# Statistics, transposes and splits of the first feed-forward pair moved up into the last attention turns

## The chip, the cores and the metric

One core of a Trainium2 chip. The time is device microseconds of one execution of the whole kernel; the median of the runs shown is compared.

## What is computed

A decoder layer on x of 4 x 2048 tokens of 512 numbers, in float32:

```python
x = x + s5(layernorm(x))                    # a linear recurrence over the 4 batch rows
x = x + cross_attention(layernorm(x), ctx)  # 16 heads, 77 context tokens for each batch row
x = x + ffn(layernorm(x))                   # 512 -> 2048, butterfly, gelu, butterfly, 2048 -> 512
```

The butterfly factors are folded into the two weight matrices of the feed-forward part while the kernel runs. Every product is made of three products of split operands: a high part that the tensor engine can take, and the low rest.

## The kernel before

The tokens are worked in NG = 16 groups of 512 (T = 4 tiles of 128 tokens). Three phases follow each other: the recurrence, attention and the feed-forward part.

**Attention** is software-pipelined in turns g = 0 to 17. Turn g makes scores and exponentials of group g, the values and half of the output projections of group g-1, the other half of group g-2, and the transposes and queries of group g+1. Each engine has its own list for a turn, written out by hand: attn_pe (TensorE, called PE), attn_act (ScalarE, ACT), attn_dve (VectorE, DVE), norm (GpSimd, POOL), and a list of DMAs on SyncE (SP). An engine works its list strictly in order, and waits on semaphores where it needs another. In turn 15 the last scores are made. Turn 16 has no scores: it has values(0) to values(3) and project(0), project(1) of group 15, and project(2), project(3) of group 14. Turn 17 has only project(2) and project(3) of group 15 with their residual additions.

Results of PE pass through four PSUM banks, 4 to 7, by slot numbers: slot n lies in bank 4 + n % 4, and PE waits until DVE has finished the slot that had the bank before (semaphore dve_slot). ACT copies the high part out (hi), DVE subtracts it and writes the low part (lo). Scores use banks 0 to 3. So values(2), slot 12, waits for lo_v(0), slot 8; turn_p(0), slot 14, waits for lo_v(1), slot 10; project(0), slot 18, waits for the low part of slot 14; project(3) (slot 7) waits for residual(2), slot 3, in the same bank.

For each tile t of group g: scores(t) on PE, shift(t) on DVE (two maxima and a subtraction), exp(t) on ACT, sums(t) on DVE (sum and reciprocal), norm on POOL, then turn_p(t) on PE (transposes), hi_p and lo_p.

**The feed-forward part** works the groups in pairs p = 0 to 7. Before its first product a pair needs: load_x2 of both groups into X; stats3(0), stats3(1) (DVE, LayerNorm statistics, L1149 and L1161 to L1167); rsqrt (POOL, L694 and L696); apply3(0), apply3(1) (ACT, L814); turn3(0) to turn3(7) (PE, 4 transposes each, L1737); raw_x(0) to raw_x(7) (ACT, L930), copying them to rawx; and seven operand splits in the order B11, T3, T2, B21, B22, T4, T1: hi_x3 (ACT, L935), lo_x3 (DVE, L1178), with mix_x (DVE, L1322) ahead of T3, T2, T4, T1. Each mix_x needs a split before it, and each hi_x3 of a mixed operand needs its mix_x. Then the products up(0, c, j) read weights from a ring of seven buffers (load_ring, L612). The third of them, A12, writes to a bank of which ACT must first have copied the first product (U, L1066), and this copy stands behind all seven hi_x3 in ACT's list.

For p = 0 all of this stands in turns 16 and 17. In turn 16 each engine works the stats, applies and transposes between its attention steps; the split of B22 comes ahead of residual(2) of turn 17 on DVE, the splits T4 and T1 come behind residual(3) of turn 17.

**Weights of the feed-forward part** are made on the way: turn g mixes, splits and stores one of 16 sets (load_wc, mix_weights L1308 and L1314, high_weights L939, low_weights L1178, store_wc L586 and L587) through one buffer pair, so that each load waits for the store before. The last set, 15, is made in turn 16. The operands B22, T4 and T1 lie where this buffer pair was, so that ACT waits for wc_stored of set 15 ahead of them; before the change ACT waits so ahead of all seven.

SP works one list as well: near the end store_x2(16), store_wc(15), a wait until that is stored, a wait for the last values, seven load_ring, store_x2(17).

## Time and profile before

| | |
|---|---|
| median of 3 runs | 2364.82 us (2364.71 to 2370.11) |
| the profiled execution | 2366.6 us, span 2364.8 us |
| TensorE busy | 2226.1 us, 94% of the span |
| VectorE busy | 1769.8 us, 75% |
| ScalarE busy | 1293.1 us, 55% |
| GpSimd busy | 557.2 us, 24% |
| attention turns 15 to 17 | about 966 to 1055 us of the span |
| first feed-forward products | from 1055 us |

PE's busy time counts matmuls whatever the clock. The granted clock (PEclk) is given as a share of full speed: 1.00 is 2.4 GHz, 0.50 is 1.2 GHz. Lines of the time line give the start in us from the span's start, the duration in us, the engine, the line, the operation with its operands, how often, and in brackets how long the engine stood idle before it and who ended the wait.

### The profile page before, as it was taken

Reading aid. Unit: us, or ns where it says so; the run is one execution under the profiler, and the core shown is the slowest. Engines: PE = TensorE matmul, PEld = TensorE weight load, DVE = VectorE, ACT = ScalarE, POOL = GpSimd, SP = SyncE. Lnnn points to the kernel's source line nnn. Section 1 sums busy time; section 2 is a strip of 40 time slices with the busy share of each in tenths; the row PEclk is TensorE's granted clock in tenths of the full one; section 3 lists DMA queues with packets and bytes.
Section 4 is the critical chain, followed back from the end, with each engine's and each line's share of the span. In section 5 each row is a group of like instructions: output and inputs, shape, how many; then the busy total and the mean of one; then the engine's idle time right before and its main releaser. Section 6 shows DMA issues by size and latency. Waiting matters only on the chain.

```text
span 2364.8 us, 42243 instructions
## 1 busy us (share of the span) xinstructions
PE 2226.1 (94%) x15752; PEld 1943.3 (82%) x15752; DVE 1769.8 (75%) x2969; ACT 1293.1 (55%) x2832; POOL 557.2 (24%) x619
## 2 busy tenths in 40 slices
PE   8877789999999999969999999999999999999998
PEld 4777668778777877748998998988989989989898
DVE  5999668878878887755875867857858758678567
ACT  2998556666667666543644635535536446355343
POOL 3788222222222322200030030020210300300203
PEclk9888879999999999989999999999999999999999
DMA  8555702332332232256568677676685686776765
GB/s 329 192 178 189 263 2 77 116 124 77 108 116 94 85 119 90 95 182 219 172 219 267 199 218 227 208 262 179 212 263 177 214 266 200 223 221 210 225 188 177
DMA packets 190883, 424.47 MB, mean 179 GB/s; under 512 B 27342, under 2 KB 64718, under 8 KB 190286
## 3 DMA queue, kind: packets, MB, share of 16 engines
q1 hardware_dynamic: 190696, 421.94, 55.1%
q8 instruction: 121, 1.98, 0.3%
q14 instruction: 66, 0.54, 0.1%
HBM read 331.29 MB, written 90.60 MB: 178 GB/s over the span
## 4 chain that ended last, share of the span: by engine, by line
PE 65%; DVE 16%; ACT 11%; issue 4%; DMA 3%; POOL 1%; SPq 0%; DVEq 0%; ACTq 0%; POOLq 0%
PE ps L416 52%; PE ps L1805 5%; ACT es L982 5%; PE ps L1773 2%; DVE gl L1178 2%; DVE G L1530 2%; DVE st L1149 2%; DVE ptl L1178 1%; DVE wc_s L1178 1%; PE ps L1784 1%; DMA xa<-in_x 1%; DVE rsum L1401 1%; ACT wc_h L939 1%; DVE rmax L1390 1%; ACT pth L957 1%
## 5 line engine op out<-in xcount | busy, mean ns | idle before, releaser
L416 PE MATMUL ps<-ring,gh 128*128 128x256 f32 x3584 | 654.4, 285 | 12.6 <-DVE gl L1178 12.5
L416 PEld LDWEIGHTS ps<-ring,gh 128*128 128x128 f32 x3584 | 558.0, 192 | 16.9 <-DVE gl L1178 15.7
L416 PE MATMUL ps<-xth,ring 128*128 128x512 f32 x1792 | 554.6, 390 | 4.2 <-ACT U L1066 4.2
L416 PE MATMUL ps<-ring,gl 128*128 128x256 f32 x1792 | 506.8, 283 | 0.0
L416 PEld LDWEIGHTS ps<-xth,ring 128*128 128x128 f32 x1792 | 337.4, 188 | 74.7 <-issue 4.6
L1054 ACT ACTIVATE gh<-G 128x512 fp32r<-128x512 f32 x384 | 237.2, 629 | 212.4 <-PE ps L416 212.1
L416 PE MATMUL ps<-xtl,ring 128*128 128x512 f32 x896 | 349.5, 390 | 0.0
L416 PEld LDWEIGHTS ps<-ring,gl 128*128 128x128 f32 x1792 | 343.4, 192 | 0.0
L1178 DVE TENSOR_TENSOR gl<-G,gh 128x512 fp32r<-128x512 f32 x384 | 278.8, 739 | 57.2 <-ACT gh L1054 55.6
L759 POOL TENSOR_TENSOR es<-es,rinv 128x308 f32<-128x308 f32 x256 | 180.2, 735 | 456.5 <-DVE rinv L1405 456.5
L1470 DVE TENSOR_TENSOR U<-ps,U 128x512 f32<-128x512 f32 (+1 forms) x168 | 137.3, 817 | 169.5 <-PE ps L416 166.9
L1037 ACT ACTIVATE G<-G,up_b 128x512 f32<-128x512 f32 x192 | 139.2, 725 | 222.1 <-DVE G L1470 222.1
L1470 DVE TENSOR_TENSOR G<-ps,U 128x512 f32<-128x512 f32 x192 | 132.8, 692 | 123.5 <-PE ps L416 122.9
L694 POOL TENSOR_TENSOR rstd<-var_e,mhalf 128x4 f32<-128x4 f32 x48 | 55.2, 1150 | 629.1 <-DVE var_e L1167 629.1
L416 PEld LDWEIGHTS ps<-xtl,ring 128*128 128x128 f32 x896 | 168.8, 188 | 34.9
L982 ACT ACTIVATE es<-ps,rmax 128x77 f32<-128x77 f32 x512 | 157.9, 338 | 60.0 <-DVE rmax L1390 60.0
L786 POOL TENSOR_TENSOR X<-X,U 128x256 f32<-128x256 f32 x64 | 72.7, 1166 | 488.4 <-DVE U L1470 488.4
L416 PE MATMUL ps<-woh,aoh 128*128 128x512 f32 x256 | 107.8, 421 | 16.0 <-DVE x L1381 12.5
L1784 PE MATMUL ps<-ident,es 128*128 128x128 f32 (+1 forms) x768 | 104.0, 284 | 19.7 <-POOL es L759 6.3
L1037 ACT ACTIVATE G<-ps,up_b 128x512 f32<-128x512 f32 x64 | 44.2, 690 | 136.7 <-PE ps L416 136.7
L957 ACT ACTIVATE pth<-ps 128x512 fp32r<-128x512 f32 x128 | 69.7, 597 | 87.7 <-PE ps L1784 87.7
L775 POOL TENSOR_TENSOR X<-X,ob 128x512 f32<-128x512 f32 x64 | 86.2, 1379 | 127.0 <-DMA X<-x_scratch 113.2
(212 smaller groups left out, 4646.0 us busy)
## 6 DMA issues: line engine op xcount, KB each, us to landing
ring<-wup_scratch SPq DMA_DIRECT2D x224, 512.0 KB, 3.8
ring<-wdn_scratch SPq DMA_DIRECT2D x224, 512.0 KB, 3.6
X<-x_scratch SPq DMA_DIRECT2D x32, 1024.0 KB, 8.5
xa<-in_x SPq DMA_DIRECT2D x16, 1024.0 KB, 5.5
x_scratch<-xa SPq DMA_DIRECT2D x16, 1024.0 KB, 4.3
x<-x_scratch SPq DMA_DIRECT2D x16, 1024.0 KB, 5.6
x_scratch<-x SPq DMA_DIRECT2D x16, 1024.0 KB, 4.3
out_x<-X SPq DMA_DIRECT2D x16, 1024.0 KB, 6.3
```

The source lines that it names most:

```text
L416: mm = pe.matmul(bank, a, b, start=first and i == 0, stop=last and i == n - 1, skip_group_check=go_on)
L759: mul = nc.gpsimd.tensor_tensor(e[:, f], e[:, f], r[:, f].unsqueeze(2).broadcast_to([P, HPC, L]), ALU.mult)
L775: x = tt(X[:, i * T + t, :], X[:, i * T + t, :], ob[:, :], ALU.add)
L786: ins = tt(x, x, U[:, u + t // 2, t % 2 * HW:(t % 2 + 1) * HW], ALU.add)
L957: his.done(A(out, bank, ACT.Copy), hi_slot(n))
L982: e = A(es[t % 2][:, f, h * L:(h + 1) * L], ps[:, h, f * LP:f * LP + L], ACT.Exp, bias=rmax[:, t % 2, at:at + 1], accum_out=rsum[:, t % 2, ...
L1037: A(dst, dst if src is None else src, ACT.Gelu, bias=up_b[:, chunk:chunk + 1]).then_inc(gelu_done, 1)
L1054: A(gh[e % GR][:, :], src, ACT.Copy).then_inc(g_hi, 1)
L1178: sub = lambda o, a, b: V.tensor_tensor(o, a, b.bitcast(F32), ALU.subtract)
L1470: add = lambda o, a, b: V.tensor_tensor(o, a, b, ALU.add)
L1784: mm = pe.transpose(b[0:keys.shape[1], j * P:(j + 1) * P], keys, ident[:, :])
L1805: mm = pe.matmul(b[0:VW[c]], v[:, f, V_AT[c]:V_AT[c + 1]], pt, start=(i == 0), stop=(i == len(passes) - 1))
```

## The change

The order on five engines is changed; no operation is added or dropped.

- Turn 15: DVE has stats3(0) behind residual(3) and stats3(1) behind sums(1). ACT has apply3(0) behind hi_v(1) and apply3(1) behind high_weights. POOL has its two rsqrt behind the norms of tiles 0 and 1.
- Turn 16, PE: turn3(0) to turn3(3) come first of all, turn3(4) to turn3(7) behind project(2). ACT: raw_x(0) to raw_x(3) ahead of hi_p(2), raw_x(4) to raw_x(7) ahead of hi_p(3), the splits B11 and T3 ahead of hi_v(0), T2 ahead of hi_v(1), high_weights right behind hi_v(1), B21 behind hi_v(3), then the wait for wc_stored, then B22, T4, T1. DVE: the low parts of B11 and T3 and two mix_x ahead of lo_v(0), T2 ahead of lo_v(1), B21 behind residual(0), B22 behind residual(1); T4 and T1 stay behind residual(3) of turn 17.
- SP: the seven load_ring are issued ahead of store_wc(15) and the wait for its end.

```diff
--- before.py
+++ after.py
@@ -621,11 +621,11 @@
             store_wc(NG - 2)
             load_wc(NG - 1)
             store_x2(NG)
-            store_wc(NG - 1)
-            sp.wait_ge(wc_stored, 32 * NG)
             sp.wait_ge(pe_slot, SLOTS * NG + V_SLOT[-1] + 1)
             for n in range(RING):
                 load_ring(n)
+            store_wc(NG - 1)
+            sp.wait_ge(wc_stored, 32 * NG)
             store_x2(NG + 1)
             sp.dma_start(ob[:, :], bcon).then_inc(ob_loaded, 16)
             sp.dma_start(ob2[:, :], dbias).then_inc(ob_loaded, 16)
@@ -758,12 +758,14 @@
                     for f in range(KC):
                         mul = nc.gpsimd.tensor_tensor(e[:, f], e[:, f], r[:, f].unsqueeze(2).broadcast_to([P, HPC, L]), ALU.mult)
                     mul.then_inc(p_ready, 1)
+                    if g == NG - 1 and t == 0:
+                        rsqrt(2 * NG, xn2_ready, NG)
+                    if g == NG - 1 and t == 1:
+                        rsqrt(2 * NG + 1, xn3_ready, 1)
 
             attn_loop(pool, norm)
 
 
-            rsqrt(2 * NG, xn2_ready, NG)
-            rsqrt(2 * NG + 1, xn3_ready, 1)
             tt = nc.gpsimd.tensor_tensor
             pool.wait_ge(ob_loaded, 32)
             tt(ob[:, :], ob[:, :], ob2[:, :], ALU.add).then_inc(ob_ready, 1)
@@ -986,31 +988,43 @@
                         e = es[t % 2][:, :, 0:HB * L]
                         A(e, e, ACT.Exp).then_inc(exp_done, 1)
 
+                if g == NG:
+                    for i in range(4):
+                        raw_x(0, i, i)
                 hi_p(2, -1)
+                if g == NG:
+                    for i in range(4, 8):
+                        raw_x(0, i, i - 4)
                 hi_p(3, -1)
                 exp(0)
                 if has(1) and not (isinstance(g, int) and g == 0):
                     apply2(g + 1)
                 if g == NG:
                     load_table(ACT.Gelu)
-                    apply3(0)
+                    act.wait_ge(x2_stored, 16 * (NG - 2))
+                    hi_x3(0, B11)
+                    hi_x3(0, T3)
                 hi_v(0)
                 hi_x(0)
                 if g == NG:
-                    apply3(1)
+                    hi_x3(0, T2)
                 exp(1)
                 hi_v(1)
+                if g == NG:
+                    high_weights(g - 1)
+                if g == NG - 1:
+                    apply3(0)
                 hi_x(1)
                 hi_v(2)
                 hi_v(3)
-                if 1 <= g <= NG:
+                if 1 <= g < NG:
                     high_weights(g - 1)
+                if g == NG - 1:
+                    apply3(1)
                 if g == NG:
-                    for i in range(8):
-                        raw_x(0, i, i % 4)
-                    act.wait_ge(x2_stored, 16 * (NG - 2))
+                    hi_x3(0, B21)
                     act.wait_ge(wc_stored, 32 * NG)
-                    for o in SPLIT_ORDER:
+                    for o in SPLIT_ORDER[4:]:
                         hi_x3(0, o)
                 if isinstance(g, int) and g == 0:
                     for j in range(4):
@@ -1408,22 +1422,25 @@
                 if has(1) and not (isinstance(g, int) and g == 0):
                     moments2(g + 1)
                 residual(2, -2)
-                if g == NG:
-                    stats3(0)
                 shift(0)
                 lo_p(3, -1)
                 sums(0)
                 residual(3, -2)
+                if g == NG - 1:
+                    stats3(0)
                 if g == NG:
-                    stats3(1)
-                if g == NG + 1:
-                    split_first(5, PROD)
+                    split_first(0, 2)
+                    mix_x(0, 1)
                 shift(1)
                 lo_v(0)
                 lo_x(0)
                 if 1 <= g <= NG:
                     mix_weights(g - 1)
                 sums(1)
+                if g == NG - 1:
+                    stats3(1)
+                if g == NG:
+                    lo_x3(0, T2)
                 lo_v(1)
                 lo_x(1)
                 lo_v(2)
@@ -1442,10 +1459,12 @@
                 sums(2)
                 lo_x(3)
                 if g == NG:
-                    split_first(0, 3)
+                    split_first(3, 4)
                 residual(1, -1)
                 if g == NG:
-                    split_first(3, 5)
+                    split_first(4, 5)
+                if g == NG + 1:
+                    split_first(5, PROD)
                 lo_p(1, 0)
                 shift(3)
                 lo_q(0)
@@ -1816,9 +1835,18 @@
                     slots.done(split3(pe, bank(O_SLOT[t]), [(aoh[:, f, tok], aol[:, f, tok], woh[:, f, :], wol[:, f, :])
                                                             for f in range(KC)]), O_SLOT[t])
 
+                if g == NG:
+                    pe.wait_ge(e_ready, T * NG)
+                    pe.wait_ge(exp_ps, T * NG)
+                    for i in range(4):
+                        turn3(0, i, i)
                 turn_p(2, -1)
                 project(2, -2)
                 scores(0)
+                if g == NG:
+                    for i in range(4):
+                        pe.wait_ge(x3_raw, i + 1)
+                        turn3(0, 4 + i, i)
                 turn_p(3, -1)
                 project(3, -2)
                 start = isinstance(g, int) and g == 0
@@ -1832,20 +1860,11 @@
                     scores(1)
                 values(2)
                 values(3)
-                if g == NG:
-                    pe.wait_ge(e_ready, T * NG)
-                    pe.wait_ge(exp_ps, T * NG)
-                    for i in range(4):
-                        turn3(0, i, i)
                 turn_p(0, 0)
                 scores(2)
                 turn_x(2)
                 project(0, -1)
                 turn_x(3)
-                if g == NG:
-                    for i in range(4):
-                        pe.wait_ge(x3_raw, i + 1)
-                        turn3(0, 4 + i, i)
                 project(1, -1)
                 turn_p(1, 0)
                 scores(3)
```

## Rows read from the trace of the kernel before

**Rows 1.** The page: shares of the chain that ended last
```profile
PE 65%; DVE 16%; ACT 11%; issue 4%; DMA 3%; POOL 1%; SPq 0%; DVEq 0%; ACTq 0%; POOLq 0%
```
**Rows 2.** Time line of PE, turns 15 to 17 (start, us, operation, idle before)
```profile
988.61 1.50 PE L1784 MATMUL ps<-ident,es 128*128 128x128 f32 x12 [2.85 <-DVE aol L1178]
...
1008.94 2.82 PE L1784 MATMUL ps<-ident,es 128*128 128x128 f32 x12 [4.74 <-POOL es L759]
...
1024.75 1.94 PE L1737 MATMUL ps<-ident,X 128*128 128x128 f32 x16
...
1049.89 0.79 PE L416 MATMUL ps<-woh,aoh 128*128 128x512 f32 x1 [12.53 <-DVE x L1381]
...
1062.64 0.69 PE L416 MATMUL ps<-xth,ring 128*128 128x512 f32 x1 [4.22 <-ACT U L1066]
```
**Rows 3.** Chain that ended last, in order of time, 1000 to 1055 (start, us, what)
```profile
1000.42 0.81 DVE rmax L1390
...
1002.98 0.84 ACT es L982 x5
...
1030.44 6.46 DMA wdn_scratch<-wc_s
...
1036.97 1.07 ACT xth L935
...
1039.29 1.15 DVE rawx L1322
...
1048.02 1.22 DVE xtl L1178
1049.24 0.61 DVE x L1381
...
1049.89 5.50 PE ps L416 x12
```
**Rows 4.** Time line of DVE, turns 15 and 16
```profile
980.93 0.68 DVE L1178 TENSOR_TENSOR aol<-ps,aoh 128x512 fp32r<-128x512 f32 x1
985.04 1.68 DVE L1308 TENSOR_TENSOR wc_s<-wc_s 128x256 f32<-128x256 f32 x4 [3.43 <-DMA wc_s<-wd_scratch]
...
989.90 1.29 DVE L1178 TENSOR_TENSOR ptl<-ps,pth 128x512 fp32r<-128x512 f32 x2 [0.25 <-ACT pth L957]
...
1008.90 2.46 DVE L1149 BATCH_NORM_STATS2 st<-X 128x6 f32<-128x512 f32 x4
...
1012.29 1.28 DVE L1178 TENSOR_TENSOR ptl<-ps,pth 128x512 fp32r<-128x512 f32 x2
```
**Rows 5.** Time line of ACT, one apply3 of turn 16
```profile
1013.88 2.94 ACT L814 ACTIVATE X<-X,nmr,rstd 128x512 f32<-128x512 f32 x4
```
**Rows 6.** DMA issues with us to landing, asked at 967.6, 1030.4 and 1040.0
```profile
wdn_scratch<-wc_s SPq DMA_DIRECT2D x1, 896.0 KB, 13.2
...
wdn_scratch<-wc_s SPq DMA_DIRECT2D x1, 896.0 KB, 6.5
...
ring<-wup_scratch SPq DMA_DIRECT2D x1, 512.0 KB, 8.4
```
**Rows 7.** Time line of SP's queue
```profile
966.04 0.92 SPq L605 DMA_DIRECT2D X<-x_scratch  x2
...
1036.92 3.34 SPq L612 DMA_DIRECT2D ring<-wup_scratch  x7
```
**Rows 8.** One stretch of 1 us: PE, PEld, DVE, ACT, POOL busy times, PEclk, DMA share, GB/s
```profile
1047.00:1048.00 1.00, 0.00 (x0) 0.00 (x0) 1.00 (x1) 0.01 (x1) 0.00 (x0) 0.50 0.44 172
```
**Rows 9.** Time line of PE, pauses of earlier turns
```profile
329.07 2.15 PE L1784 MATMUL ps<-ident,es 128*128 128x128 f32 x9 [2.55 <-DVE ptl L1178]
521.41 0.76 PE L1805 MATMUL ps<-pth,vh 128*128 128x512 f32 x1 [3.35 <-issue]
```
**Rows 10.** Stretches of 1 us, as rows 8: the clock behind two pauses
```profile
989.00:990.00 1.00, 1.00 (x11) 0.84 (x8) 0.75 (x3) 0.73 (x2) 1.00 (x3) 1.00 0.00 0
...
1013.00:1014.00 1.00, 1.00 (x4) 0.81 (x3) 0.97 (x2) 0.99 (x3) 0.77 (x2) 0.50 0.03 8
```

## The prediction

> **What bounds the kernel.** I read the page first: PE is busy for 94% of the span (in the table above) and holds 65% of the chain that ended last [rows 1]. So an edit is worth only what it does to PE's pauses and to its clock. I then read PE's time line over the turns that the diff touches. There the reader sees a pause of 2.85 us in turn 15, one of 4.74 us at 1008.94, one of 12.53 us at 1049.89 that DVE's residual addition ended, and one of 4.22 us at 1062.64 that ACT's copy U ended [rows 2]. These are what the change can win. The chain of this stretch [rows 3] tells why the long one exists: the store of weight set 15 lands at 1036.90, then come five splits in turns of ACT and DVE, the last low part at 1048.02 and residual(2) of turn 17 at 1049.24, and only then may project(3) start in the same bank. It starts at 1049.89 and takes 5.50 us, at half clock. Third come the clock and the DMA rows, since both are about to be loaded differently.
>
> What decides is the start of this last project(3). Behind it nothing is moved: it ends at 1055.39, residual(3), mix_x, T4, mix_x, T1 and U follow, and the third product starts at 1062.64 [rows 2, 3], 7.25 us later. From there on PE runs the same work as before. So the effect of the whole change is the shift of that start.
>
> **Turn 15, what is added.** One stats3 holds DVE from 1008.90 to 1012.29, 3.39 us [rows 4]. The first sits ahead of shift(1), so lo_v(0), at 980.93 before, comes 3.4 us later. values(2) had followed it at once and now waits some 3.3 us. mix_weights stood idle for its DMA until 985.04 [rows 4] and absorbs the lateness of DVE: this DMA does not move. The second stats3 has no such cover: it sits between sums(1) and lo_v(1), and turn_p(0) waits for the latter [rows 2], so 988.61 becomes 992.0. ACT now has two apply3 of 2.94 us [rows 5] in turn 15, the second ahead of hi_p(0). Its statistics end at 991.3, POOL's rsqrt takes some 1.3 us more, apply3(1) ends at 995.5, and hi_p(0) and lo_p(0), which was at 989.90 [rows 4], come at 996.1: 6.2 us late. project(0) and shift(2) wait for that. Slack in the rest of the turn returns some 0.7 us. I get the end of scores(3) at 1005.4, where it was at 1000.0: 5.4 us late. The X loads are issued at 966.04 [rows 7] and landed long before DVE wants them.
>
> **Turn 16.** The first turn3 use the scores' banks and so wait for exp(3): from its maximum to the last exponential out of these banks tile 3 took from 1000.42 to 1003.82, 3.4 us [rows 3]. PE stands from 1005.3 to 1008.7, 3.4 us. The old order had turn_p(2) and project(2) there and then 4.74 us of pause for the norm of tile 3 [rows 2]; that pause is gone, since 16 transposes (1.94 us [rows 2]), turn_p(2), project(2) and again 16 transposes cover it. With 1.4 us for a turn_p (1.50 with its tail [rows 2]) and 2.8 for a project (half of the 5.50 at half clock [rows 3]), values(0) starts at 1020.8, against 1015.9. Next is values(2): it waits for lo_v(0), behind B11, mix_x, T3, mix_x. Table load until 1020.2, then 1.07 (hi) + 1.22 (low) + 1.15 (mix) + 1.07 + 1.22 + 1.15 [rows 3] and about 1 for aoh and aol: 1028.1. PE pauses 3.6 us, and values(3) ends at 1032.0, where it ended at 1024.8: 7.2 us late. The last low_weights ends at 1035.4 instead of 1029.8, 5.6 us late.
>
> **The DMA order.** This is the step that I think decides. SP issues the seven ring loads at 1032.0 and needs 3.34 us [rows 7], then at 1035.4 the stores of set 15. In the trace, the seventh ring load was issued at about 1040.0 and landed 8.4 us later [rows 6], 1048.3; the DMA share of 0.44 in the microsecond of 1047 [rows 8] puts the last of their bytes at about 1047.4, 10.5 us behind the first issue. Does a store queued behind them wait for them? At 967.6 the trace has that very case: set 13's store was queued behind the two X loads of 966.04 and took 13.2 us to land, against 6.5 us when nothing was ahead of it [rows 6, 7]. So it waits. Alone, the second half of the store landed 6.46 us behind its issue [rows 3] and the whole 7.1 us behind the first; of that about 1.1 us passed before bytes moved, as an estimate from the ring loads (issued at 1036.92, done 10.5 us later), so 6.0 us are left behind a full queue. wc_stored then comes at 1032.0 + 10.5 + 6.0 = 1048.5. Before it was 1036.90: 11.6 us later, although its data are only 5.6 us later.
>
> The Trainium skill (DMA: Bandwidth & Descriptors, section Queues, rings and completion order) says that each DMA engine takes the descriptors of one ring in order and shares its time only between different queue rows. That speaks against this change, as the landing of 13.2 us does.
>
> **What the splits give back.** Four of seven splits are now out of the way early, but B22 still waits for wc_stored and still stands ahead of residual(2) of turn 17. So 1048.5 + 1.1 (hi) + 1.2 (low) + 0.7 (residual and issue) gives project(3) at 1051.5; carried through with the same small issue gaps as before, the shift against 1049.89 lies between +1.4 and +2.2 us. I take +2. The pause ahead of it is about 9.5 us instead of 12.53, and the clock is low behind it in both. The ends of this term: were the store as fast as at 1030.44 (7.1 us from issue), project(3) would start at 1045.5, -4.4 us; with a receipt as slow as at 967.6, +3.3 us.
>
> **The clock.** Removed is the half clock behind the pause of 4.74 us: turn_p(3) took 2.82 us instead of 1.50 [rows 2] and the clock was still 0.50 at 1013 [rows 10]. That saving is already in my times above, which are all at full clock. Added are two pauses where PE then sets the pace, 3.4 us at 1008.7 and 3.6 us at 1028.1. Pauses of 2.55 and 3.35 us were followed by half clock: nine transposes took 2.15 us [rows 9], where twelve take 1.50 [rows 2], and a first matmul of values 0.76; one of 2.85 us was not, twelve took 1.50 and the clock at 989 was 1.00 [rows 2, 10]. Behind 1008.94 the clock was still 0.50 at 1013 [rows 10], in all some 6 us; so a pause costs between 0 and 3 us. I take 1.7 for each, 3.4 in all: something past the middle, since two of the three pauses of this size brought half clock. In turn 15 the pauses lie under DVE's lateness and cost at most 0.7 us.
>
> The Trainium skill (TensorE: Matmul & The Clock Gate, section What's actually happening) says that the monitor behind the clock runs free of the kernel, so whether a given pause costs anything is partly chance. By that the two terms are 0 or full; the sum would be +2, +3.7 or +5.4 us.
>
> **The sum.** +2.0 + 3.4 = +5.4 us on the profiled execution: span 2364.8 to 2370.2, time 2366.6 to 2372.0. The median of the runs is 2364.82, so 2370.2 there. A measurement of this kernel can tell some 0.3%, 7.1 us, from no change; the forecast lies inside.
>
> **Rivals.**
> - *The store is not held up* (for: it is a smaller transfer, and some of its bytes may overtake; against: the 13.2 us of rows 6). Then B22 is split at 1045 and project(3) starts 4.4 us earlier than before, less the 0 to 3.4 us of clock: 2360.4 to 2363.8. Chance 0.15.
> - *The pauses cost more* (slower): each of the two at 1008.7 and 1028.1 leaves the clock at 0.50 for 6 us, as at 1008.94, and turn 15's 0.7 us counts: 2.0 + 6.0 + 0.7 = +8.7, 2373.5. It decides once half clock outlasts 5 us behind each pause. Chance 0.25.
> - *Turn 15 hides the statistics*: DVE had 3.43 us of idle ahead of mix_weights [rows 4], and if hi_p(0) is not the late one, scores(3) is only 1 to 2 us late. T3 and T2 come earlier, the ring loads start 4 us earlier, and everything behind them: -4 + 5.4, 2366 or, with full clock, 2363. Chance 0.1.
> - *The change pays as it looks*: both of the above together, the 12.53 us pause falls to 2 or 3 us: about -9, 2356. Chance 0.05.
> - My forecast, 2368 to 2372: 0.45.
>
> The range drops the last rival and the far end of the second: 2360 to 2375. Faster by over 0.3%: 0.07; within: 0.63; slower: 0.30.
>
> **What would show it.** Right: scores(3) of group 15 ends 4 to 6 us later; DVE's BATCH_NORM_STATS2 lies ahead of the second and behind the second shift of turn 15; ring loads are issued at about 1032 to 1036, the stores of set 15 land 12 to 14 us after their issue; the long pause of PE is still ahead of a projection, ended by DVE's addition, some 9 us, and ACT stands about 15 us for that DMA. Wrong: a landing of 7 us for these stores, project(3) starting before 1047, full clock behind the pauses of 3.5 us, or turn_p(0) of turn 15 ahead of 990.

## The result, and the profile after

The changed kernel takes 2373.97 us in the median of six runs (2370.83 to 2375.76), against 2366.30 us for six runs of the kernel before beside it (2364.62 to 2370.11). The ratio is 1.0028, 95% interval 1.0015 to 1.0040: slower by 0.28%, just below what I had called the limit of what can be told. A second set of runs of the same kernel, with 17 runs of the kernel before beside it, gave 2374.5 us and 1.0038 (1.0025 to 1.0050). So by the medians the change costs 7.7 and 8.4 us; the two intervals reach from 3.5 to 12 us. The forecast was 2370.2 us, between 2360 and 2375. It was worked out from 2364.82 us, the median of three runs of the kernel before; from the 2366.30 of six the same shift of 5.4 us gives 2371.7.

The page of the changed kernel: busy times, and the chain's shares. No busy time has moved by more than 1.3 us, and PE's by 0.3 (rows 1 had the chain), so the eight microseconds are nearly all waiting.

```profile
span 2373.0 us, 42244 instructions
PE 2226.4 (94%) x15752; PEld 1942.0 (82%) x15752; DVE 1769.4 (75%) x2969; ACT 1292.3 (54%) x2832; POOL 556.3 (23%) x619
PE 64%; DVE 17%; ACT 9%; issue 4%; DMA 4%; DVEq 0%; SPq 0%; POOL 0%; ACTq 0%; POOLq 0%
```

PE's time line of the changed kernel, to be laid beside [rows 2] (start, duration, operation, idle before it and who ended it). The line numbers have moved: L1803 is turn_p, L1756 turn3, L1824 values.

```profile
985.06 0.50 PE L1824 MATMUL ps<-pth,vh 128*128 128x512 f32 x1 [2.98 <-DVE aol L1192]
...
992.13 1.50 PE L1803 MATMUL ps<-ident,es 128*128 128x128 f32 x12 [3.12 <-DVE aol L1192]
...
997.15 0.67 PE L416 MATMUL ps<-woh,aoh 128*128 128x512 f32 x1 [2.05 <-DVE ptl L1192]
...
1011.16 3.47 PE L1756 MATMUL ps<-ident,X 128*128 128x128 f32 x16 [3.91 <-issue]
...
1056.99 0.80 PE L416 MATMUL ps<-woh,aoh 128*128 128x512 f32 x1 [10.06 <-DVE x L1395]
...
1069.62 0.77 PE L416 MATMUL ps<-xth,ring 128*128 128x512 f32 x1 [4.50 <-ACT U L1080]
```

The pause of 4.74 us has gone and three shorter ones, of 2.98, 3.12 and 2.05 us, have come in turn 15, one of 3.91 us at the head of turn 16, and (not shown) one of 3.52 us ahead of values(2). The long pause is still ahead of the last project(3), still ended by DVE's addition, 10.06 us instead of 12.53. The third product starts at 1069.62, 6.98 us later than before. The span is 8.2 us longer. Turn 15 starts at 965.8 to 965.9 in both traces, and from the third product to the end they take 1302.2 and 1303.4 us, so all but 1.2 us of it lies in this stretch. PE's pauses in the stretch (those the time line shows, 0.4 us and more) add up to 32.1 us, where they were 26.4: 5.7 of the 6.9 us. The rest is work that took longer.

The chain that ended last, of the changed kernel, against [rows 3] (start, duration, what):

```profile
1040.53 0.56 SPq L586
1041.09 0.04 issue
1041.13 12.87 DMA wdn_scratch<-wc_s
1054.03 1.06 ACT xth L937
1055.12 0.03 DVE xtl L1192
1055.15 1.11 issue
1056.26 0.69 DVE x L1395
1056.95 0.04 issue
1056.99 5.39 PE ps L416 x12
```

The store's 6.46 us have become 12.87, and between it and project(3) there is now one split where there were five.

### The profile page after: what moved, and what is told of

It is laid out like the page before. It is cut to its first block, busy times and chain, and to the rows that moved or that the text cites. A ratio compares the mean times of both kernels' runs of the same rounds, so it can differ in the third digit from the quotient of the medians.

```text
span 2373.0 us, 42244 instructions
## 1 busy us (share of the span) xinstructions
PE 2226.4 (94%) x15752; PEld 1942.0 (82%) x15752; DVE 1769.4 (75%) x2969; ACT 1292.3 (54%) x2832; POOL 556.3 (23%) x619
## 4 chain that ended last, share of the span: by engine, by line
PE 64%; DVE 17%; ACT 9%; issue 4%; DMA 4%; DVEq 0%; SPq 0%; POOL 0%; ACTq 0%; POOLq 0%
PE ps L416 52%; PE ps L1824 5%; ACT es L984 5%; DVE st L1163 2%; PE ps L1792 2%; DVE gl L1192 2%; DMA xa<-in_x 2%; DVE G L1549 2%; DVE ptl L1192 2%; DMA x_scratch<-xa 1%; PE ps L1803 1%; DVE wc_s L1192 1%; DVE rsum L1415 1%; DVE rmax L1404 1%; ACT pth L959 1%
## 5 line engine op out<-in xcount | busy, mean ns | idle before, releaser
L416 PEld LDWEIGHTS ps<-ring,gh 128*128 128x128 f32 x3584 | 558.0, 192 | 16.9 <-DVE gl L1192 15.6
L416 PEld LDWEIGHTS ps<-xth,ring 128*128 128x128 f32 x1792 | 338.0, 189 | 75.4 <-issue 4.9
L416 PE MATMUL ps<-woh,aoh 128*128 128x512 f32 x256 | 107.6, 420 | 16.6 <-DVE x L1395 10.1
L1803 PE MATMUL ps<-ident,es 128*128 128x128 f32 (+1 forms) x768 | 102.4, 281 | 15.1 <-DVE xt2l L1192 5.7
```

The source lines that it names most:

```text
L416: mm = pe.matmul(bank, a, b, start=first and i == 0, stop=last and i == n - 1, skip_group_check=go_on)
L1803: mm = pe.transpose(b[0:keys.shape[1], j * P:(j + 1) * P], keys, ident[:, :])
```

## The experiments

Single traces differ in where turn 15 starts (962.8 to 965.9 us), so I read each trace from the start of its turn_p(2) of turn 15, called 0 here. "Landed" is the landing of the store of set 15, "third" the start of the third product (where the copy U is early, the pause is at another product, and no number is given). The experiments were run in three sets; the median of the kernel before beside them was 2366.00, 2366.23 and 2366.12 us, and 2366.30 beside the changed kernel's first.

| kernel | scores(3) end | landed | third | median us | ratio to before (95%) |
|---|---|---|---|---|---|
| before | 34.2 | 71.1 | 96.8 | 2366.0 to 2366.3 | 1 |
| changed | 41.4 | 88.1 | 103.8 | 2373.97 | 1.0028 (1.0015 to 1.0040) |
| store first | 41.2 | 81.4 | 96.1 | 2365.5 | 0.9998 (0.9987 to 1.0008) |
| B22 late | 41.2 | 88.0 | 96.8 | 2368.13 | 1.0006 (0.9996 to 1.0016) |
| ring first alone | 37.6 | 80.8 | 106.5 | 2373.24 | 1.0026 (1.0014 to 1.0039) |
| statistics alone | 41.2 | 75.4 | 100.4 | 2370.82 | 1.0022 (1.0013 to 1.0032) |
| both orders | 41.3 | 81.4 | 93.1 | 2362.80 | 0.9986 (0.9978 to 0.9995) |
| residuals first | 34.1 | 70.6 | 93.5 | 2364.64 | 0.9994 (0.9986 to 1.0003) |
| statistics placed | 40.7 | 88.0 | 103.7 | 2374.18 | 1.0038 (1.0024 to 1.0051) |
| placed, both orders | 40.6 | 81.5 | 93.1 | 2362.25 | 0.9985 (0.9976 to 0.9993) |
| placed, both orders, U early | 40.6 | 81.4 | - | 2359.89 | 0.9974 (0.9965 to 0.9984) |
| before, residuals first, U early | 34.2 | 70.7 | - | 2359.60 | 0.9974 (0.9963 to 0.9985) |
| changed, again | 41.6 | 90.0 | 104.6 | 2374.50 | 1.0038 (1.0025 to 1.0050) |

**1. The store ahead of the ring loads again.** The changed kernel with one edit on SP:

```diff
-            sp.wait_ge(pe_slot, SLOTS * NG + V_SLOT[-1] + 1)
-            for n in range(RING):
-                load_ring(n)
             store_wc(NG - 1)
             sp.wait_ge(wc_stored, 32 * NG)
+            sp.wait_ge(pe_slot, SLOTS * NG + V_SLOT[-1] + 1)
+            for n in range(RING):
+                load_ring(n)
```

> The changed kernel with SP's old order: store of weight set 15 and the wait for it ahead of the seven ring loads. Theory (the store queued behind the ring loads decides the end): the stores are issued when low_weights ends, about 1040.5, and land in 7.1 us instead of 13, at 1047.6; B22, residual(2) follow, the last project(3) starts at 1050.6 instead of 1057.0, the third product 6.4 us earlier; 6 to 7 us faster than the changed kernel, 0 to 2 us slower than the kernel before. Rival (the chain of splits or the clock holds project(3) back whatever the store does): no change against the changed kernel, 7 to 8 us slower than before.

Measured: 2365.5 us, 8.5 us less than the changed kernel and level with the kernel before. Its chain, in the same form as above:

```profile
1040.83 6.43 DMA wdn_scratch<-wc_s
...
1047.29 1.06 ACT xth L937
...
1049.52 0.69 DVE x L1395
...
1050.25 4.46 PE ps L416 x12
```

The second half of the store takes 6.43 us instead of 12.87; project(3) starts at 1050.25 where 1050.6 was expected. The low weights are ready at nearly the same time in both kernels (DVE ends them at 1040.15 here and at 1040.43 there; the first half of the store is issued at 1040.23 and 1040.53), so the 6.4 us are the place in the queue and nothing else. The third product starts 7.7 us earlier than in the changed kernel: the rest is mostly project(3), which took 4.46 us here and 5.39 there. The rival is out.

**2. B22 behind the last residual.** The changed kernel with one edit on DVE:

```diff
-                if g == NG:
-                    split_first(4, 5)
                 if g == NG + 1:
-                    split_first(5, PROD)
+                    split_first(4, PROD)
```

> The changed kernel with the low part of B22 behind residual(3) of turn 17 instead of ahead of residual(2); SP's new order is kept, so the store still lands late, about 1054. Theory (what costs is that residual(2), and with it project(3), stands behind a split that waits for the store): project(3) follows project(2) without a pause at 1047, full clock; PE's pause moves behind the first two products, which end near 1053; B22, T4, T1 and U follow the store in some 9 us, so the third product starts at about 1063 instead of 1069.6: 6 to 7 us faster than the changed kernel. Rival (the end is the store's landing plus a fixed chain): the third product stays at 1068 to 1070 and nothing is gained.

Measured: 2368.13 us, 5.8 us less than the changed kernel. In PE's time line the pause has moved from project(3) to the third product:

```profile
1045.93 0.50 PE L416 MATMUL ps<-woh,aoh 128*128 128x512 f32 x1 [0.85 <-DVE x L1395]
...
1061.11 0.76 PE L416 MATMUL ps<-xth,ring 128*128 128x512 f32 x1 [9.41 <-ACT U L1080]
```

From the store's landing to the third product it takes 8.8 us; in the changed kernel it takes 15.6, since project(3) stood in between. The store was as late as before. So the late store costs what it does because two residuals stand behind a split that needs it.

**3. The ring loads first, alone.** The kernel before with the edit of experiment 1 the other way round.

> The kernel before with only SP's new order: seven ring loads ahead of the store of set 15. Theory (DMA queue in order): ring loads are issued at 1024.9 when the last values end, the store is issued at 1029.8 and lands some 16.8 us behind the first ring load, at 1041.7 instead of 1036.9; all seven splits, project(3) and the third product come 4.8 us later: +5 us on the whole. Rival (the queue shares its time between transfers): the store lands as before or within 2 us, +0 to +2 us.

Measured: 2373.24 us, 7.2 us slower than before: the SP order by itself costs as much as the whole change. DMA issues of this kernel, asked at 1031.5 and 1032.1 (KB, us to landing):

```profile
wdn_scratch<-wc_h SPq DMA_DIRECT2D x1, 896.0 KB, 11.3
wdn_scratch<-wc_s SPq DMA_DIRECT2D x1, 896.0 KB, 13.2
```

From the first ring load at 1026.57 to the landing at 1045.28 it took 18.7 us, 1.9 more than in the changed kernel and more than the 16.8 I had expected. In the microseconds from 1043 and 1044 only 24 and 23 GB/s were moved, where it had been about 385 before; why the end of the store dragged here is not shown. The rival, a queue that shares its time, forecast a landing at most 2 us later and is out. The changed kernel's own trace agrees: its seventh ring load, issued at 1040.05, landed 9.2 us later, against 8.4 us with no store behind it [rows 6], and the store landed 4.8 us after that.

The trace of experiment 3 also has a thing that has nothing to do with the edit: its turn 15 is 3.4 us longer than in the trace of before, though the instructions are the same. PE's time line and two stretches show why (in each stretch: its length, the busy time of PE, PEld, DVE, ACT and POOL with their instructions, then the granted clock, the DMA share and GB/s):

```profile
987.52 1.50 PE L1784 MATMUL ps<-ident,es 128*128 128x128 f32 x12 [3.09 <-DVE aol L1178]
```

```profile
988.00:989.00 1.00, 1.00 (x14) 0.80 (x12) 0.75 (x2) 0.82 (x2) 1.00 (x3) 0.94 0.00 0
...
992.00:993.00 1.00, 1.00 (x3) 0.81 (x3) 1.00 (x2) 0.37 (x3) 0.00 (x0) 0.50 0.00 0
```

The pause was 3.09 us here and 2.85 us there [rows 2], and here 1.2 GHz followed it for some 7 us, where there the clock stayed at 2.4 GHz [rows 10]. Of these 3.4 us 2.9 are left where the store is issued (67.0 us from the start of turn 15, against 64.0), so some 3 of this trace's 9.7 us at the third product come from the clock in turn 15, and 6.7 are the order.

**4. The statistics in turn 15, alone.** The kernel before with the moves on DVE, ACT and POOL that bring the statistics forward, and nothing else (the added lines; the same calls are taken out of turn 16):

```diff
@@ POOL, turn 15
+                    if g == NG - 1 and t == 0:
+                        rsqrt(2 * NG, xn2_ready, NG)
+                    if g == NG - 1 and t == 1:
+                        rsqrt(2 * NG + 1, xn3_ready, 1)
...
@@ ACT
                 hi_v(1)
+                if g == NG - 1:
+                    apply3(0)
...
                     high_weights(g - 1)
+                if g == NG - 1:
+                    apply3(1)
...
@@ DVE
                 residual(3, -2)
+                if g == NG - 1:
+                    stats3(0)
...
                 sums(1)
+                if g == NG - 1:
+                    stats3(1)
```

> The kernel before with only the statistics, rsqrt and apply3 of both groups moved into turn 15; transposes, splits and SP's order stay. Theory (turn 15 is paced by DVE and ACT, which is what the statistics load): the end of scores(3) of group 15 moves from 1000.0 to 1007.2, as in the changed kernel; turn 16 wins back some 2 us since apply3(1) no longer stands ahead of high_weights; the store lands at about 1042 and the third product starts 4 to 6 us later: +5 us. Rival (the statistics hide beside DMA waits and slack of turn 15): scores(3) at most 2 us later, and a gain of 1 to 3 us on the whole.

Measured: 2370.82 us, 4.8 us slower. scores(3) ends 7.0 us later, as in the changed kernel, so turn 15's whole lateness is the statistics. Turn 16 gives back a little more than expected (the store lands 4.3 us later, the third product starts 3.6 us later, where 4 to 6 had been forecast). The rival is out.

**5. Both orders.** Experiments 1 and 2 in one kernel.

> The changed kernel with both repairs: SP stores set 15 ahead of the ring loads, and B22 is split behind residual(3) of turn 17. Theory (the store's late landing and the residuals behind it are one chain, and what is left after the first repair is the store's own landing plus hi B22, mix, T4, mix, T1, U): the store lands at 1047.3 as in the first repair; from the landing to the third product the second repair took 8.8 us, so it starts at 1056.1 instead of 1062.0; 6 us faster than the first repair alone, 6 to 7 us (0.3%) faster than the kernel before. Rival (the two repairs remove the same wait and do not add): no more than 1 us better than the better of the two.

Measured: 2362.8 us, 2.7 us less than with the first repair alone and 3.4 us (0.14%) less than before, where 6 to 7 were expected. The third product starts 3.0 us earlier than with the first repair, not 6. What I had overlooked is in PE's time line:

```profile
1047.21 0.50 PE L416 MATMUL ps<-woh,aoh 128*128 128x512 f32 x1 [0.85 <-DVE x L1395]
...
1050.65 0.50 PE L416 MATMUL ps<-xth,ring 128*128 128x512 f32 x1 [0.40 <-DMA ring<-wup_scratch]
...
1058.64 0.76 PE L416 MATMUL ps<-xth,ring 128*128 128x512 f32 x1 [4.97 <-ACT U L1080]
```

B22's low part stands behind residual(3), and residual(3) waits for project(3), which ends at 1050.25. In experiment 2 the store landed after that, and the 8.8 us began with the landing; here the landing is at 1047 and the chain begins with project(3), so 3 of the 6 us are taken back. The chain that ended last says the same: it runs through project(3) and residual(3), and the store is no longer in it.

**6. Residuals first in the kernel before.** One edit on DVE: of the seven splits only the first stays ahead of the residuals of turn 17.

```diff
                 residual(3, -2)
...
                 if g == NG + 1:
-                    split_first(5, PROD)
+                    lo_x3(0, T3)
+                    split_first(2, PROD)
...
-                if g == NG:
-                    split_first(0, 3)
                 residual(1, -1)
                 if g == NG:
-                    split_first(3, 5)
+                    split_first(0, 1)
+                    mix_x(0, 0)
```

> The kernel before with one edit: on DVE the two residual additions of turn 17 come right behind the first split and mix_x, and the other six splits behind them. Theory (the pause of 12.53 us before the last project(3) is owed to the order on DVE alone, not to statistics or transposes): project(3) follows project(2) at about 1039 after some 1 to 2 us of pause instead of 12.5, the splits run on beside it, the third product starts at about 1056 instead of 1062.6; 6 to 7 us faster than the kernel before. Rival (the chain of seven splits is as long as the pause, so nothing is won by letting project(3) go): within 2 us of before.

Measured: 2364.64 us, 1.6 us less than before, and the interval (0.9986 to 1.0003) takes in no change. The trace's third product is 3.3 us earlier. project(3) has its pause cut from 12.53 to 3.68 us, but the second product now waits 4.14 us for T2 and the third 6.41 us for U. So the rival was right on the time, but the trace gives another reason than its own. The edit puts both residuals ahead of the splits, and residual(3) waits for project(3). So the splits did not run on beside project(3), as I had expected; the chain that ended last goes through all of it:

```profile
1039.84 4.61 PE ps L416 x12
...
1044.54 0.12 DVE x L1381
...
1045.15 1.22 DVE xtl L1178
```

Up to 1044.54 DVE was idle for 4.76 us, and ACT for 7.25 us up to its next split, while the third product waited for the splits that DVE had still to work. It is the same wait as in experiment 5. An order with only residual(2) ahead of the splits and residual(3) behind some of them was not tried.

**7. The statistics in other places of turn 15.** The changed kernel; stats3(0) into DVE's wait for the weights, stats3(1) behind the low parts that free PE's banks, apply3(1) behind hi_p(0).

```diff
                 residual(3, -2)
-                if g == NG - 1:
-                    stats3(0)
...
                 lo_x(0)
+                if g == NG - 1:
+                    stats3(0)
                 if 1 <= g <= NG:
                     mix_weights(g - 1)
                 sums(1)
-                if g == NG - 1:
-                    stats3(1)
...
                 lo_v(3)
+                if g == NG - 1:
+                    stats3(1)
...
@@ ACT
-                if g == NG - 1:
-                    apply3(1)
...
                 hi_p(0, 0)
+                if g == NG - 1:
+                    apply3(1)
```

> The changed kernel with the statistics in other places of turn 15: stats3(0) ahead of mix_weights, where DVE stood 3.4 us idle for a DMA, stats3(1) behind lo_v(3), apply3(1) behind hi_p(0). SP's order and the splits stay as changed. Theory (turn 15's 7 us are owed to where the statistics and apply3(1) stand, not to their amount): the end of scores(3) comes back from 1007.2 to about 1003.5, and all behind it 3 to 4 us earlier: 3 to 4 us faster than the changed kernel. Rival (DVE and ACT are full in turn 15, any place costs the same 6.8 us): no change.

Measured: 2374.18 us, no change against the changed kernel; scores(3) ends 0.7 us earlier in the trace, not 3 to 4. PE's time line:

```profile
985.38 1.06 PE L1803 MATMUL ps<-ident,es 128*128 128x128 f32 x8 [2.72 <-DVE aol L1192]
...
987.85 1.06 PE L1803 MATMUL ps<-ident,es 128*66 128x128 f32 x4 [1.40 <-DVE aol L1192]
...
992.52 0.76 PE L416 MATMUL ps<-woh,aoh 128*128 128x512 f32 x1 [0.90 <-DVE ptl L1192]
```

The pauses are shorter, 5.0 us in three instead of 8.2. The clock took nearly all of it back. It fell at 987, behind the first of them, and stayed at 0.50 for some 10 us, where the changed kernel had it so for some 3 us from 997 on. So the transposes of turn_p(0) took 2.1 us instead of 1.5, scores(2) 2.79 instead of 1.54, project(0) and project(1) 8.11 instead of 7.32: from the start of turn 15 to the end of scores(3) PE's work took 2.4 us more in all, against 3.1 us less pause, and 0.7 us are left. In the traces of experiments 8 and 9, which have the same places, the pauses, the 10 us of half clock and the end of scores(3) (40.6) are the same. My theory was that the place and not the amount costs the time. The place did change the pauses; in the time it gained nothing.

**8. All three repairs.** Experiments 5 and 7 in one kernel.

> All three repairs in the changed kernel: statistics in the idle places of turn 15, store ahead of the ring loads, B22 behind residual(3) of turn 17. Theory (the causes are independent and add): third product 3 to 4 us earlier than with the two orders repaired, 9 to 10 us (0.4%) faster than the kernel before, 16 to 18 us faster than the changed kernel. Rival (once the store is not late, turn 16's own chain takes over): no better than the two orders alone.

Measured: 2362.25 us, as experiment 5 (2362.8). That is 4.0 us less than before and 11.7 less than the changed kernel, where 9 to 10 and 16 to 18 had been forecast. The other places of the statistics give nothing here either: scores(3) ends 0.7 us earlier than in experiment 5, the store lands at the same time (81.5 against 81.4), and so does the third product start (93.1). The rival held.

**9. The copy U early.** Experiment 8, and on ACT the high parts of T4 and T1 behind the copy U in the first round of the products.

```diff
-                    for o in SPLIT_ORDER[4:]:
+                    for o in SPLIT_ORDER[4:5]:
                         hi_x3(0, o)
...
                     A(U[:, 2 - 2 * (c % 2)], ps[:, 4 * (c % 2) + UP_BANK[A11], :], ACT.Copy).then_inc(first_copied, 1)
+                    if p == 0 and c == 0:
+                        for o in SPLIT_ORDER[5:]:
+                            hi_x3(0, o)
```

> The version with all three repairs, and on ACT the copy U of the first product (on which the third product waits) ahead of the high parts of T4 and T1 instead of behind them. Theory (after the repairs what PE waits for longest is the copy U, 4.7 us, which stands behind the chain of splits only by its place in ACT's list): the third product starts some 0.5 us after the second ends, two products (2.7 us) are made while T4 and T1 are split, and the fifth waits for T1 till about 59.5 where it was at 61.1: 1.5 to 2.5 us faster than the three repairs alone. Rival (the last split T1 is needed by the fifth product at about the time at which it is ready anyway): within 0.5 us of it.

Measured: 2359.89 us, 2.4 us less than experiment 8 and 6.2 us (0.26%, interval 0.16 to 0.35%) less than the kernel before. Four products run through without a stop, and the pause, now 2.96 us, is ahead of the fifth.

**10. The copy U and the residuals, in the kernel before.** Experiment 6 with the edit of experiment 9.

> The kernel before with the residuals of turn 17 first on DVE, and with the copy U ahead of the high parts of T4 and T1 on ACT; statistics, transposes and SP's order as before. Theory (the whole gain that was in this stretch lies in two places of the order, and none in moving the statistics): the pause of 6.4 us ahead of the third product shrinks, the fifth product starts some 2 us earlier than with the residuals alone: 5 to 6 us faster than the kernel before, as good as the changed kernel with all its repairs. Rival (without the early statistics and splits the chain of seven splits is the bound and the copy gives nothing): as with the residuals alone, 1 to 3 us faster than before.

Measured: 2359.6 us, 6.5 us less than the kernel before, level with experiment 9, which has the statistics, transposes and splits moved, the three repairs and the same copy. Its time line of PE:

```profile
1040.76 0.50 PE L416 MATMUL ps<-woh,aoh 128*128 128x512 f32 x1 [3.69 <-DVE x L1384]
...
1050.90 0.50 PE L416 MATMUL ps<-xth,ring 128*128 128x512 f32 x1 [4.14 <-DVE xtl L1181]
...
1060.30 0.47 PE L416 MATMUL ps<-xth,ring 128*128 128x512 f32 x1 [3.41 <-issue]
```

The lines are the last project(3), the second product and the fifth. DVE waits for project(3) here as in experiment 6, 4.77 us. Against experiment 6 the median gains 5.0 us, more than the 2 us that the chain was expected to give. There a pause of 6.41 us was followed by half clock, here one of 3.41 us was not. One stretch of each (numbers as in experiment 3), experiment 6 first. It is one trace of each, so that the clock makes up the difference is likely and not shown.

```profile
1061.00:1062.00 1.00, 1.00 (x4) 0.81 (x3) 0.00 (x0) 0.43 (x1) 0.00 (x0) 0.50 0.00 0
```

```profile
1061.00:1062.00 1.00, 1.00 (x5) 0.69 (x5) 0.65 (x2) 0.00 (x0) 0.00 (x0) 1.00 0.00 0
```

**11. The changed kernel again.**

> The changed kernel itself once more, on the chip and in the rounds of the two others, for an interval of its own and a second trace. Expected: 7 to 8 us slower than the kernel before; the store behind the ring loads lands 12 to 13 us after its issue again; the pauses of 3.0, 3.1 and 3.5 us in turns 15 and 16 are there at the same places, but which of them is followed by half clock differs from the first trace. Rival (the half clock behind each pause is fixed by the program): the same stretches at 0.50 as in the first trace.

Measured: 2374.5 us, 8.4 us more than the kernel before beside it, ratio 1.0038. The second half of the store landed 12.8 us after its issue. The pauses are at the same places. Ahead of turn_p(0) of turn 15 the pause is 3.55 us, followed by half clock, where it was 3.12 us and full clock. scores(2) then took 2.78 us instead of 1.54, but the next pause shrank from 2.05 to 0.46 us, and the clock was half at project(0) in both traces; scores(3) ends at 41.6 and 41.4. Ahead of values(2) of turn 16 the pause is 3.54 us (3.52 in the first trace). The clock was still 1.00 in the first microsecond behind it and half for some 3.5 us after that, so values(2) and values(3) took 5.5 us, no less than the first trace's 5.4. So the rival fell, but the draw changed little in the time.

```profile
992.00:993.00 1.00, 1.00 (x12) 0.59 (x14) 0.00 (x0) 1.00 (x3) 0.00 (x0) 0.50 0.00 0
...
1031.00:1032.00 1.00, 0.41 (x2) 0.37 (x3) 0.97 (x3) 0.97 (x2) 0.00 (x0) 1.00 0.00 0
```

## Why the prediction was right, and where it was off

The direction, the mechanism and the range held; the size was 5.4 us forecast against 7.7 measured. The narrower band that I held most likely, 2368 to 2372, was missed: the median is 2 us above it. Of the signs that were to show the forecast right, the store's landing (13.5 us behind its issue, 12 to 14 forecast), the long pause (10.06 us, some 9) and ACT's wait for the DMA (15.37 us, about 15) came; scores(3) ended 7.2 us late, where 4 to 6 had been said, and the ring loads were issued at 1037.2, outside 1032 to 1036. None of the signs for wrong came.

The shift of the third product can be taken apart by the traces of before and after, both read from the start of turn 15:

| term | before | after | difference | forecast |
|---|---|---|---|---|
| turn 15 start to store issued | 64.0 | 74.7 | +10.6 | +9.0 (5.6 + 3.4 for the clock) |
| store issued to landed | 7.1 | 13.5 | +6.4 | +6.0 |
| landed to third product | 25.7 | 15.6 | -10.1 | -10.0 |
| sum | 96.8 | 103.8 | +6.9 | +5.4 |

The three terms of the forecast sum to +5.0 and not to its +5.4, because it took +2 for a shift that its own terms put at 1.6 without the clock. Against +6.9 its sum is 1.5 us too small, and the first term accounts for that.

- **Turn 15, the amount.** Forecast 5.4 us at the end of scores(3), measured 7.2. The steps behind it held: values(2) waited 2.98 us (about 3.3 forecast), turn_p(0) started at 992.13 (992.0), hi_p(0) at 995.70 and lo_p(0) at 996.31 (996.1), and project(0) started at 997.15, right behind. What was mis-sized is the clock in turn 15, which the forecast put at 0.7 us at most and left out of its sum. Behind the pause of 2.05 us ahead of project(0) the clock was at 0.50 at 998, and project(0) and project(1) took 7.32 us instead of the 5.7 that they took before: 1.6 us. I had looked at each pause alone and taken the last one, 2 us, for too short; three pauses in 15 us were not the same thing. It was no bad luck of one trace: in all six traces with the statistics in these places the clock was half at project(0), whichever of the pauses it had fallen behind, the two projections took 7.1 to 7.3 us, and scores(3) ended at 41.2 to 41.6. Experiment 4 confirms that the whole lateness is the statistics.
- **Turn 16.** The pause ahead of the first turn3 was 3.91 us (3.4 forecast), the one ahead of values(2) 3.52 (3.6). Both were followed by half clock, as assumed: 16 transposes took 3.47 us instead of 1.94, and values(2) and values(3) 5.4 instead of 4.0. Together 2.9 us, where 3.4 had been taken. Here I had weighed two outcomes for each pause; all eight traces that have these two pauses show half clock behind both.
- **The DMA order.** Forecast: landing 16.5 us behind the first ring load. Measured 1054.0 - 1037.2 = 16.8. Experiment 1 shows that the price of the order is 6.4 us at the landing, 7.7 us at the third product and 8.5 us in the medians, experiment 3 that the order costs 7.2 us with nothing else changed. That is shown, not only argued.
- **What the splits give back.** Shown by experiment 1: with the store issued 10.3 us later than before it still reaches the third product 0.8 us earlier. In round numbers the moved splits are worth 10 us of chain; the statistics that make them possible cost 7, turn 16's own pauses 3, the store's place 6.
- **The rival "the pauses cost more"** stood at 2373.5, nearer to the result than the forecast. It was right that the clock cost more, but not where it said: behind the two pauses in turn 16 the half clock lasted 3 to 4 us in the first trace, not 6; the missing part came in turn 15. (In experiment 11 it did last 5.7 us behind the first of them.) **"The store is not held up"** is refuted by experiments 1 and 3, **"turn 15 hides the statistics"** by experiments 4 and 7, and so is **"the change pays as it looks"**.

What stays open: why the clock falls behind one pause and not behind another of the same length, and the last microsecond between the trace (6.9) and the medians (7.7 and 8.4). Medians of the kernel before differ by up to 1.5 us (2364.82 for the first three runs, 2366.0 to 2366.3 for the larger sets).

## What to carry to other kernels

A step moved early is paid for where it lands: before moving, look for the queue of each engine that it joins and for what waits behind it, and price the short pauses with the clock that may follow them. A wait on a store must be costed with all transfers that are issued ahead of that store in its queue, and nothing that the bound engine needs should stand behind the work that has such a wait. And look first for the waits that the order alone makes: two moves of a few lines in the kernel before (residuals ahead of splits, one copy ahead of two splits) gave 6.5 us, as much as the whole rearrangement with its three repairs and the same copy. Last, an operation that itself waits for the bound engine holds up all that stands behind it in its list (experiments 5 and 6): moved ahead, it can cost what it was to win.

## What the runs showed of the hardware

- Transfers issued behind others on one queue waited for nearly all of them. The store's two halves (1.8 MB) were issued behind 3.7 MB of ring loads; the second half landed 12.9 us after its issue, 12.8 in three more traces (experiments 2, 7 and 11: 12.84, 12.89 and 12.80) and 13.2 in experiment 3, against 6.4 to 6.5 us with nothing ahead.
- The clock behind a pause of TensorE of about 3 us went either way. The work behind pauses of 2.83 to 2.85 us (before, experiments 6 and 10), 2.96 (experiment 9) and 3.41 us (experiment 10) ran at 2.4 GHz; behind 3.09 us (experiment 3) the clock went to 1.2 GHz. At one and the same place, ahead of values(2) of turn 15 with a pause of 2.98 to 3.00 us, 2.4 GHz lasted to the next pause in four traces, and the clock fell about 1.5 us behind the pause in two (experiments 2 and 4). At the next place, 3.11 to 3.12 us, it held in one trace and fell in two (experiments 1 and 5). The pauses of 3.5 to 3.9 us in turns 15 to 17 were followed by 1.2 GHz every time, at once or within about 1.5 us.
- What 1.2 GHz costs depends on what sets the next start. Ahead of another wait it cost nothing: in experiments 2 and 4 values(2) and values(3) of turn 15 took 5.5 us instead of 3.95, and the next pause shrank from 3.12 to 1.56 us. Where TensorE set the pace it cost 1.3 to 1.7 us behind each pause in turns 15 and 16 of the changed kernel and its variants, and 3.4 us in turn 15 of experiment 3.
- The runs of one kernel spread over 2 us (experiment 10, seven runs) to 11 us (the kernel before, 27 runs). That the clock makes this spread is likely from these traces, but was not shown.
